# Slot bias carried by the logits weights, and the weights prepared inside the attention stage

## The chip, the cores and the metric

The kernel runs on one core of one Trainium2 chip. The time is the device time of one execution in microseconds. Before the change three executions took 1048.29, 1049.57 and 1051.22 us, median 1049.57. The engines are named as in the profile: PE (TensorE), DVE (VectorE), ACT (ScalarE), POOL (GpSimd) and SP (SyncE, which here only issues transfers). A name such as SPq is an engine's queue of issues.

## The reference

Images are cut into 36 patches of 768 numbers and embedded into 256 features, 77 text tokens are put behind them, and then come an attention layer and a soft mixture of experts, each with a layernorm and a residual:

```python
h = patches @ W.T + b                       # 32 x 36 x 256
h = concatenate([h, txt], axis=1)           # 32 x 113 x 256
h = h + attention(layernorm(h))             # 16 heads of 16, rotary embedding
x = layernorm(h)
logits = x @ phi_w.T + phi_b                # 3616 tokens x 64 experts x 32 slots
D = softmax(logits over the 32 slots)
C = softmax(logits over the 64 experts)
X = D^T x, clipped, normalised, tanh        # 2048 slots x 256
Y = X @ expert_w + expert_b                 # per expert
out = h + C Y
```

`phi_w` is 2048 x 256 and `phi_b` has 2048 entries (one bias for each slot of each expert).

## The kernel before, in words

The program has three stages, each a block of its own with a barrier behind it: no engine begins a stage before all engines and all awaited transfers of the last are done.

`embed` multiplies the patches, nine tiles of 128 rows. While it runs, ACT issues the loads of the weights of the later stages: the query-key, value and output projections and `phi`, which arrives as 128 partitions of 2 x 2048 numbers (KC = 2 halves of 128 features). Each of these is split into two parts, a high part rounded to fp32r by ACT (`hi`, L126) and the rest (`lo`): POOL computes it at L133, and for the second half of `phi` DVE does at L170. DVE also prepares the slot bias here: L161, L164 and L165 put its high part in row 0 and its low part in row 32 of `bias_rows`, whose other rows are zero. Behind each embedded tile DVE adds the token bias (L157) and SP stores the tile (L113). The block ends when the stores have landed and the split weights are there.

`attend` handles one batch element of 113 tokens per step, in a software pipeline: in step b element b+3 is normalised, b+2 is projected to queries and keys, b+1 is turned (transposed for the scores), b is scored, b-1 is finished and b-2 gets its residual. The first steps, b = -3 to 2, are written out, and then comes a loop. Within a step every engine follows its own fixed order. POOL's is: variance plus epsilon (L383), inverse root (L385), then the sums of the rotary embedding into `attend_stack` (L395). DVE's normalisation (L339) waits for L385, and it stands ahead of the rotary products (L347, L350) in DVE's order. PE transposes the normalised rows (L551) behind it. SP loads the input rows of an element, 36 from the embedding and 77 from the text, two steps ahead, each load waiting for L339 to be done with the buffer it refills.

`slots` handles 29 tiles (the first of 32 tokens, the others of 128). For a tile PE computes the logits in four banks of 512 columns: per bank one product of `bias_ones` with `bias_rows` (L1115) and six products of the two halves of the high and low parts (L1118). For the first five tiles (`early`) all four banks stand ahead of the group products (L1092) in PE's order; after that they are woven between the transposes of the weights (L1083). DVE takes the maxima (L811), subtracts them (L816), sums (L800, L845) and collects the products (L792, L794); POOL subtracts and scales whole tiles (L929, L933, L937); ACT copies and exponentiates. Behind the tiles come the experts and the combination of the outputs.

Of the kernel before, what the change touches and what calls it, by code (L numbers as in the profile page):

```python
# [29 lines left out]
KC = C // 128  # L30
# [46 lines left out]
def embed(nc, patches, wt, bias_row, emb, loads, identity, ident, slot_bias_row, bias_rows, bias_ones):  # L77
# [4 lines left out]
    with ExitStack() as ctx:  # L82
# [7 lines left out]
        slot_raw, slot_hi = sb("slot_raw", [64, E]), sb("slot_hi", [64, E], F32R)  # L90
# [3 lines left out]
        ident_in, slot_in = sem("ident_in"), sem("slot_in")  # L94
        slot_zero_ok, slot_hi_ok, slot_ok = sem("slot_zero_ok"), sem("slot_hi_ok"), sem("slot_ok")
        raw_in = [sem(f"raw_in{n}") for n in range(len(loads))]
        hi_done, lo_done, half_done = sem("hi_done"), sem("lo_done"), sem("half_done")
# [19 lines left out]
        @block.scalar  # L117
        def _(act):
            act.wait_ge(px_in[tiles - 2], 16)
            act.dma_start(slot_raw[:], slot_bias_row.broadcast_to([64, E])).then_inc(slot_in, 16)  # L120
            act.dma_start(ident[:], identity).then_inc(ident_in, 16)
            for n, (src, _, _) in enumerate(loads):
                act.dma_start(raw[n][:], src).then_inc(raw_in[n], 16)
            for n, (_, hi, _) in enumerate(loads):
                act.wait_ge(raw_in[n], 16)
                nc.scalar.activation(hi[:], raw[n][:], ACT.Copy).then_inc(hi_done, 1)  # L126

        @block.gpsimd
        def _(pool):
            for n, (_, hi, lo) in enumerate(loads):  # L130
                pool.wait_ge(hi_done, n + 1)
                part = slice(0, KC // 2) if n == len(loads) - 1 else slice(0, KC)
                nc.gpsimd.tensor_tensor(lo[:, part], raw[n][:, part], hi[:, part].bitcast(F32),  # L133
                                        ALU.subtract).then_inc(lo_done, 1)
            pool.wait_ge(lo_done, len(loads))
# [38 lines left out]

def attend(nc, emb, txt, rope_cos, rope_sin, ident, wqk, wv, wo, h2):
# [8 lines left out]
    with ExitStack() as ctx:  # L184
# [28 lines left out]

        p_score = pb("p_score", [T, GH, 512])
# [11 lines left out]
        tables_in = sem("tables_in")  # L226
        h_ld = [sem("h_ld0"), sem("h_ld1")]
# [37 lines left out]
        def _(sp):  # L265
# [7 lines left out]
            sp.dma_start(sin[:], rope_sin).then_inc(tables_in, 16)  # L273

# [95 lines left out]
        def _(pool):  # L370
# [8 lines left out]
            def step(b, half, par, flags):  # L379
# [18 lines left out]
            steps(pool, step)  # L398
            pool.wait_ge(stack_ok, 2 * BATCH)

        @block.scalar
        def _(act):
# [9 lines left out]
            def step(b, half, par, flags):  # L412
# [152 lines left out]
def slots(nc, h2, phi, slot_bias, ident, xacc, eb, y_parts, ct_dram, ebias, wexp, w_slots, out):  # L565
# [6 lines left out]
    bias_rows, bias_ones = slot_bias  # L572
    with ExitStack() as ctx:
# [15 lines left out]
        xn = [sb(f"xn{i}", [128, C]) for i in range(2)]  # L589
# [22 lines left out]
        xst = [t[:].rearrange("p (k c) -> p k c", k=KC) for t in xn]  # L612
# [155 lines left out]
        def _(dve):  # L768
            nc.vector.memset(eps[:], EPS)
            nc.vector.memset(e_power[:], -0.5)  # L770
            nc.vector.memset(power[:], -0.5).then_inc(consts, 1)
# [8 lines left out]
            def norm_end(n, par, rows):  # L780
# [3 lines left out]
                nc.vector.tensor_scalar(xn[par][0:rows], h_t[par][0:rows], mv[0:rows, 0:1], rstd[0:rows],  # L784
# [186 lines left out]
        def _(act):  # L971
# [9 lines left out]
            def step(t, half, c):  # L981
# [9 lines left out]
                if live:  # L991
# [3 lines left out]
                    nc.scalar.activation(x[c % RING][0:rows], xn[c % 2][0:rows], ACT.Copy).then_inc(kept_ok, 1)  # L995
# [66 lines left out]
        def _(pe):  # L1062
            def turn_x(t, c, nrows):
# [3 lines left out]
                for k in range(KC):  # L1067
                    last = nc.tensor.transpose(p_turn[0][:, k, 0:nrows], xn[(c + 1) % 2][0:nrows, 128 * k:128 * k + 128],
# [38 lines left out]
            def multiply_logits(t, nrows, banks):  # L1107

                pe.wait_ge(xt_lo_ok, val(t + 2))
                for b in banks:  # L1110
# [97 lines left out]
def program(nc, patches, txt, wt, tok_b, wqk, wv, wo, phi, phi_b, wexp, ebias, rope_cos, rope_sin, identity, out):  # L1208
# [7 lines left out]
    with (nc.sbuf_tensor("ident", [128, 128], F32) as ident, ExitStack() as whole):  # L1216
# [7 lines left out]
        bias_rows = whole.enter_context(nc.sbuf_tensor("bias_rows", [128, E], F32R))  # L1224
        bias_ones = whole.enter_context(nc.sbuf_tensor("bias_ones", [128, 128], F32R))
        with ExitStack() as projections:
# [3 lines left out]
            embed(nc, patches, wt, tok_b, emb, [(wqk, *wqk_parts), (wv, *wv_parts), (wo, *wo_parts),  # L1230
                                                (phi, *phi_parts)], identity, ident, phi_b, bias_rows, bias_ones)
            attend(nc, emb, txt, rope_cos, rope_sin, ident, wqk_parts, wv_parts, wo_parts, h2)
        slots(nc, h2, phi_parts, (bias_rows, bias_ones), ident, xacc, eb, y_parts, ct, ebias, wexp, w_slots, out)
# [41 lines left out]
```

## Time and profile before

| what | value |
| --- | --- |
| median of 3 runs | 1049.57 us |
| the profiled execution, its own time | 1050.74 us |
| its span, first to last instruction | 1049.0 us |
| busy: PE, DVE, ACT, POOL | 953.9, 752.7, 483.3, 459.6 us |
| mean granted TensorE clock, 1.00 being 2.4 GHz | 0.958 |
| moved by transfers | 110.42 MB |

The durations below come from that one profiled execution, whose own time is 1.74 us more than its span and 1.17 us more than the median. Busy shares are means over stages with different limits, so each stage has to be read by itself: `embed` ends near 42 us, `attend` near 340, the tiles of `slots` near 814. Matmuls are pipelined, so that PE reads as busy also where each product merely overlaps the next.

### The profile page before, as it was taken

How to read it: one execution, taken by the hardware profiler on the slowest of the kernel's cores; microseconds unless marked ns; L12 is line 12 of the kernel's file. 1: busy time of each engine (PE TensorE's matmuls, PEld its weight loads, DVE VectorE, ACT ScalarE, POOL GpSimd, SP SyncE). 2: the span in 40 equal slices, each digit the busy share in tenths (PEclk: the TensorE clock that was granted, in tenths of full speed). 3: DMA queues.
4: the chain of work that ended last, by engine and by line, in shares of the span. 5: the costliest groups of instructions: out<-in, count | busy, mean ns of one | idle time of the engine just before them, and what ended most of it. 6: DMA issues, size and time to landing. Idle time of an engine off the chain costs nothing.

```text
span 1049.0 us, 22748 instructions
## 1 busy us (share of the span) xinstructions
PE 953.9 (91%) x8338; PEld 809.2 (77%) x8338; DVE 752.7 (72%) x1095; ACT 483.3 (46%) x768; POOL 459.6 (44%) x375
## 2 busy tenths in 40 slices
PE   7389999999997558799999999999998997999997
PEld 6278888887885346688887888888887756999997
DVE  1746767667663398899998999999998553544442
ACT  1145555555553144565565565566556233333331
POOL 0422222222220077687786787777777341010100
PEclk9689999999998788999999999999999998999999
DMA  9201111111110402223323223323325894776660
GB/s 303 73 21 36 42 42 42 40 41 40 41 33 29 103 10 56 58 79 92 80 61 88 68 67 90 82 60 86 91 62 180 318 410 145 236 224 240 220 201 23
DMA packets 97688, 110.42 MB, mean 105 GB/s; under 512 B 12148, under 2 KB 88980, under 8 KB 91684
## 3 DMA queue, kind: packets, MB, share of 16 engines
q1 hardware_dynamic: 95460, 102.31, 31.7%
q10 hardware_dynamic: 800, 3.74, 1.0%
q0 software_dynamic: 1376, 3.70, 0.9%
q8 instruction: 29, 0.48, 0.2%
q14 instruction: 23, 0.19, 0.1%
HBM read 71.51 MB, written 38.21 MB: 105 GB/s over the span
## 4 chain that ended last, share of the span: by engine, by line
DVE 26%; PE 24%; issue 11%; POOL 3%; ACT 2%; DVEq 0%; DMA 0%; POOLq 0%; ACTq 0%
PE slots_p_turn L1200 15%; DVE slots_dmax L811 6%; DVE slots_csum L800 6%; DVE slots_dsum L845 5%; PE slots_p_sum L1092 3%; DVE slots_disp L816 3%; PE slots_logits L1118 3%; DVE xacc L794 3%; ACT slots_comb L1004 1%; PE slots_logits L1167 1%; POOL slots_comb L929 1%; POOL slots_disp L933 1%; DVE slots_xn L784 1%; DVE slots_xt_lo L828 1%; DVE slots_cmax L839 1%
## 5 line engine op out<-in xcount | busy, mean ns | idle before, releaser
L1092 PE MATMUL slots_p_sum<-slots_x,slots_disp 128*128 128x256 f32 (+1 forms) x928 | 208.1, 382 | 6.1 <-POOL slots_disp L933 6.1
L1092 PEld LDWEIGHTS slots_p_sum<-slots_x,slots_disp 128*128 128x128 f32 (+1 forms) x928 | 174.6, 191 | 31.3 <-POOL slots_disp L933 4.7
L937 POOL TENSOR_TENSOR slots_comb<-slots_comb,slots_csum 128x2048 f32<-128x2048 f32 (+1 forms) x29 | 105.0, 3619 | 66.0 <-DVE slots_csum L802 66.0
L929 POOL TENSOR_TENSOR slots_comb<-slots_comb,slots_cmax 128x1024 f32<-128x1024 f32 (+1 forms) x58 | 112.0, 1949 | 44.1 <-DVE slots_cmax L839 44.1
L933 POOL TENSOR_TENSOR slots_disp<-slots_disp,slots_dsum 128x2048 f32<-128x2048 f32 (+1 forms) x29 | 105.8, 3647 | 0.0
L1004 ACT ACTIVATE slots_comb<-slots_logits 128x512 f32<-128x512 f32 (+1 forms) x116 | 66.1, 598 | 85.3 <-DVE slots_disp L816 85.3
L816 DVE TENSOR_TENSOR slots_disp<-slots_logits,slots_dmax 128x512 f32<-128x512 f32 (+1 forms) x116 | 80.2, 691 | 5.9 <-issue 1.9
L964 POOL DMA_DIRECT2D out<-slots_o x29 | 15.9, 548 | 156.3 <-DVE slots_o L899 156.3
L395 POOL TENSOR_TENSOR attend_stack<-attend_rope_a,attend_rope_b 113x256 f32<-113x256 f32 x64 | 45.3, 729 | 88.9 <-DVE attend_rope_b L350 88.9
L978 ACT ACTIVATE slots_ct<-slots_p_turn 128x512 f32<-128x512 f32 (+1 forms) x116 | 64.1, 580 | 38.7 <-PE slots_p_turn L1083 38.6
L811 DVE TENSOR_REDUCE slots_dmax<-slots_logits 128x16 f32<-128x512 f32 (+1 forms) x116 | 78.8, 679 | 3.3 <-PE slots_logits L1118 1.8
L989 ACT ACTIVATE slots_comb<-slots_comb 128x1024 f32<-128x1024 f32 (+1 forms) x58 | 61.5, 1060 | 33.4 <-POOL slots_comb L929 33.3
L1118 PE MATMUL slots_logits<-phi_hi,slots_xt_hi 128*128 128x512 f32 (+1 forms) x232 | 75.6, 408 | 0.0
L1118 PE MATMUL slots_logits<-phi_hi,slots_xt_lo 128*128 128x512 f32 (+1 forms) x232 | 75.3, 407 | 0.0
L1118 PE MATMUL slots_logits<-phi_lo,slots_xt_hi 128*128 128x512 f32 (+1 forms) x232 | 74.9, 405 | 0.0
L311 DVE TENSOR_REDUCE attend_stack<-attend_p_score 113x16 f32<-113x1808 f32 x32 | 65.4, 2043 | 13.2 <-PE attend_p_score L459 13.2
L1115 PE MATMUL slots_logits<-bias_rows,bias_ones 128*128 128x512 f32 (+1 forms) x116 | 54.4, 469 | 19.3 <-DVE slots_xt_lo L828 18.2
L409 ACT ACTIVATE attend_prob_t<-attend_p_score 113x904 f32<-113x904 f32 x64 | 55.7, 923 | 28.7 <-PE attend_p_score L468 28.7
L800 DVE TENSOR_REDUCE slots_csum<-slots_comb 128x32 f32<-128x2048 f32 (+1 forms) x29 | 66.0, 2277 | 3.3 <-ACT slots_comb L989 3.3
L839 DVE TENSOR_REDUCE slots_cmax<-slots_comb 128x32 f32<-128x2048 f32 (+1 forms) x29 | 66.3, 2286 | 2.8 <-ACT slots_comb L1004 1.3
L1083 PE MATMUL slots_p_turn<-ident,slots_comb 128*128 128x128 f32 (+1 forms) x464 | 63.7, 272 | 2.6 <-POOL slots_comb L937 1.5
L845 DVE TENSOR_REDUCE slots_dsum<-slots_disp 128x64 f32<-128x2048 f32 (+1 forms) x29 | 66.1, 2279 | 0.0
(132 smaller groups left out, 1973.6 us busy)
## 6 DMA issues: line engine op xcount, KB each, us to landing
combine_t<-slots_ct SPq DMA_DIRECT2D x224, 128.0 KB, 2.4
slots_comb<-combine_t SPq DMA_DIRECT2D x14, 1024.0 KB, 5.6
slots_ct<-combine_t SPq DMA_DIRECT2D x14, 1024.0 KB, 5.8
expert_w<-wexp SPq DMA_DIRECT2D x8, 1024.0 KB, 9.1
slots_disp<-wexp SPq DMA_DIRECT2D x8, 1024.0 KB, 13.4
h<-attend_h_out SPq DMA_DIRECT2D x32, 113.0 KB
slots_h_t<-h SPq DMA_DIRECT2D x28, 128.0 KB, 2.2
slots_x<-h SPq DMA_DIRECT2D x28, 128.0 KB, 2.0
```

The lines of the kernel that those rows point to most:

```text
L800: nc.vector.reduce_sum(csum[0:rows, 0], comb[par % 2][0:rows], AX_X).then_inc(csum_ok, 1)
L811: nc.vector.reduce_max(dmax[0:rows, bank(b)], logits[0:rows, bank(b), :], AX_X).then_inc(dmax_ok, 1)
L816: nc.vector.tensor_tensor(disp[c % RING][0:rows, bank(b), :], logits[0:rows, bank(b), :], dmax[0:rows, bank(b)].unsqueeze(2).broadcast_to( ...
L839: nc.vector.reduce_max(cmax[0:rows], comb[c % 2][0:rows], AX_X).then_inc(cmax_ok, 1)
L845: nc.vector.reduce_sum(dsum[0:rows, 0], disp[c % RING][0:rows], AX_X).then_inc(dsum_ok, 1)
L929: nc.gpsimd.tensor_tensor(m, m, cmax[0:rows, shalf(i)].unsqueeze(2).broadcast_to([rows, SLOTS // 2, EXPERTS]), ALU.subtract).then_inc(csub ...
L933: nc.gpsimd.tensor_tensor(d, d, dsum[0:rows, 1].unsqueeze(2).broadcast_to([rows, EXPERTS, SLOTS]), ALU.mult).then_inc(disp_ok, 1)
L937: nc.gpsimd.tensor_tensor(m, m, csum[0:rows, 1].unsqueeze(2).broadcast_to([rows, SLOTS, EXPERTS]), ALU.mult).then_inc(comb_ok, 1)
L1004: nc.scalar.activation(comb[c % 2][0:rows, :, bank(b)], logits[0:rows, bank(b), :].rearrange("p n s -> p s n"), ACT.Copy).then_inc(copied_ ...
L1092: last = nc.tensor.matmul(p_sum[u % 2][:, i, :], disp[d][0:rows].rearrange("p n s -> p (n s)")[:, 128 * e:128 * e + 128], x[d][0:rows], st ...
L1118: last = nc.tensor.matmul(out_b, a[:, k, 0:nrows], wt[:, k, cols], start=False, stop=i == 2 and k == KC - 1)
L1200: last = nc.tensor.matmul(p_o[c % 2][0:rows], a[c % 2][:, e, 0:rows], part[:, e, :], start=k == 0, stop=k == 3 * EB - 1)
```

## The change

The normalised token row has mean zero over its 256 features, so the first feature is minus the sum of the others. Subtracting the weights of the first feature from all the others therefore lets the first feature be left out of the product. The 255 remaining features and a column of ones make 256 rows again, and the weight row that meets the ones is the slot bias. `xn` in `slots` gets a 257th column of ones, the transposes read columns 1 to 256, and the product of the bias is gone, with `bias_rows`, `bias_ones` and all that filled them.

The weights `phi` are no longer loaded and split in `embed`. In `attend` SP loads them, shifted by one feature: 127 partitions of 16 KB, two single rows (feature 128 and the bias) into partition 127, and the row of the first feature broadcast over 128 partitions. In steps -2 to 1 POOL subtracts the first row from a quarter of the weights, at the end of a step ACT rounds the high part of a quarter (steps -1 to 2), and POOL subtracts for the low part (steps -1 to 2). POOL's first subtraction waits for all four transfers.

```diff
@@ embed
-            act.dma_start(slot_raw[:], slot_bias_row.broadcast_to([64, E])).then_inc(slot_in, 16)
             act.dma_start(ident[:], identity).then_inc(ident_in, 16)
...
-                part = slice(0, KC // 2) if n == len(loads) - 1 else slice(0, KC)
-                nc.gpsimd.tensor_tensor(lo[:, part], raw[n][:, part], hi[:, part].bitcast(F32),
-                                        ALU.subtract).then_inc(lo_done, 1)
+                nc.gpsimd.tensor_tensor(lo[:], raw[n][:], hi[:].bitcast(F32), ALU.subtract).then_inc(lo_done, 1)
...
-            nc.vector.memset(bias_rows[:].bitcast(F32), 0.0)
-            nc.vector.memset(bias_ones[:].bitcast(F32), 1.0).then_inc(slot_zero_ok, 1)
...
-                if t == tiles - 3:
-
-                    dve.wait_ge(slot_in, 16)
-                    nc.vector.tensor_copy(slot_hi[:], slot_raw[:]).then_inc(slot_hi_ok, 1)
-                    dve.wait_ge(slot_hi_ok, 1)
-                    dve.wait_ge(slot_zero_ok, 1)
-                    nc.vector.tensor_copy(bias_rows[0:1], slot_raw[0:1]).then_inc(slot_ok, 1)
-                    nc.vector.tensor_tensor(bias_rows[32:33], slot_raw[32:33], slot_hi[32:33].bitcast(F32),
-                                            ALU.subtract).then_inc(slot_ok, 1)
-            dve.wait_ge(slot_ok, 2)
-            dve.wait_ge(hi_done, len(loads))
-            _, hi, lo = loads[-1]
-            nc.vector.tensor_tensor(lo[:, KC // 2:KC], raw[-1][:, KC // 2:KC], hi[:, KC // 2:KC].bitcast(F32),
-                                    ALU.subtract).then_inc(half_done, 1)
-            dve.wait_ge(half_done, 1)
@@ attend
+        PIECES = 4
+        piece = lambda t, i: t[:].rearrange("p k e -> p (k e)")[:, i * KC * E // PIECES:(i + 1) * KC * E // PIECES]
...
             sp.dma_start(sin[:], rope_sin).then_inc(tables_in, 16)
+            sp.dma_start(phi_raw[0:127], phi[1:128]).then_inc(phi_in, 16)
+            sp.dma_start(phi_raw[127:128, 0], phi[0:1, 1]).then_inc(phi_in, 16)
+            sp.dma_start(phi_raw[127:128, 1], slot_bias).then_inc(phi_in, 16)
+            sp.dma_start(phi_first[:], phi[0:1, 0].broadcast_to([128, E])).then_inc(phi_in, 16)
...
+                if isinstance(b, int) and -2 <= b < PIECES - 2:
+
+
+                    pool.wait_ge(phi_in, 64)
+                    i = b + 2
+                    rows = slice(0, 128 if i < PIECES // KC else 127)
+                    part = slice(i * KC * E // PIECES % E, i * KC * E // PIECES % E + KC * E // PIECES)
+                    nc.gpsimd.tensor_tensor(piece(phi_raw, i)[rows], piece(phi_raw, i)[rows], phi_first[rows, part],
+                                            ALU.subtract).then_inc(phi_sub_ok, 1)
+                if isinstance(b, int) and -1 <= b < PIECES - 1:
+
+                    pool.wait_ge(phi_hi_ok, b + 2)
+                    nc.gpsimd.tensor_tensor(piece(phi_lo, b + 1), piece(phi_raw, b + 1), piece(phi_hi, b + 1).bitcast(F32),
+                                            ALU.subtract).then_inc(phi_lo_ok, 1)
...
+                if isinstance(b, int) and -1 <= b < PIECES - 1:
+
+                    act.wait_ge(phi_sub_ok, b + 2)
+                    nc.scalar.activation(piece(phi_hi, b + 1), piece(phi_raw, b + 1), ACT.Copy).then_inc(phi_hi_ok, 1)
@@ slots
-        xn = [sb(f"xn{i}", [128, C]) for i in range(2)]
+        xn = [sb(f"xn{i}", [128, C + 1]) for i in range(2)]
...
+            for i in range(2):
+                nc.vector.memset(xn[i][:, C:C + 1], 1.0)
...
-                    last = nc.tensor.transpose(p_turn[0][:, k, 0:nrows], xn[(c + 1) % 2][0:nrows, 128 * k:128 * k + 128],
+                    last = nc.tensor.transpose(p_turn[0][:, k, 0:nrows], xn[(c + 1) % 2][0:nrows, 128 * k + 1:128 * k + 129],
                                                ident[0:nrows, 0:nrows])
...
-                    nc.tensor.matmul(out_b, bias_ones[:, 0:nrows], bias_rows[:, cols], start=True, stop=False)
                     for i, (a, wt) in enumerate(((xt_hi, phi_hi), (xt_hi, phi_lo), (xt_lo, phi_hi))):
                         for k in range(KC):
-                            last = nc.tensor.matmul(out_b, a[:, k, 0:nrows], wt[:, k, cols], start=False,
+                            last = nc.tensor.matmul(out_b, a[:, k, 0:nrows], wt[:, k, cols], start=i == 0 and k == 0,
                                                     stop=i == 2 and k == KC - 1)
```

What SP issues at the start of `attend` in the changed kernel, in its order (`attend_h_in` are the input rows, a bracket names the semaphore that an issue waits for):

```order
L256 DMA attend_cos<-rope_cos 113x16
L257 DMA attend_sin<-rope_sin 113x16
L258 DMA attend_phi_raw<-phi 127x4096
L259 DMA attend_phi_raw<-phi 1x2048
L260 DMA attend_phi_raw<-phi_b 1x2048
L261 DMA attend_phi_first<-phi 128x2048
L251 DMA attend_h_in<-emb 36x256 [waits attend_xn_ok]
L252 DMA attend_h_in<-txt 77x256
```

The four issues with `phi` are new and stand ahead of the loads of elements 2 and 3. Before the change the loads stood directly behind the two tables.

What POOL has in steps -2 and -1 in the kernel before (`attend_mv` and `attend_rstd` are the variance and inverse root of the element to be normalised):

```order
L383 TENSOR_TENSOR attend_mv<-attend_mv,attend_eps 113x1 [waits attend_mv_ok]
L385 TENSOR_TENSOR attend_rstd<-attend_mv,attend_power 113x1 [waits attend_var_ok]
L395 TENSOR_TENSOR attend_stack<-attend_rope_a,attend_rope_b 113x4x4x16 [waits attend_rope_ok]
L395 TENSOR_TENSOR attend_stack<-attend_rope_a,attend_rope_b 113x4x4x16
L383 TENSOR_TENSOR attend_mv<-attend_mv,attend_eps 113x1 [waits attend_mv_ok]
L385 TENSOR_TENSOR attend_rstd<-attend_mv,attend_power 113x1 [waits attend_var_ok]
L395 TENSOR_TENSOR attend_stack<-attend_rope_a,attend_rope_b 113x4x4x16 [waits attend_rope_ok]
```

And in the changed kernel, in the same steps and the start of step 0:

```order
L371 TENSOR_TENSOR attend_mv<-attend_mv,attend_eps 113x1 [waits attend_mv_ok]
L373 TENSOR_TENSOR attend_rstd<-attend_mv,attend_power 113x1 [waits attend_var_ok]
L383 TENSOR_TENSOR attend_stack<-attend_rope_a,attend_rope_b 113x4x4x16 [waits attend_rope_ok]
L383 TENSOR_TENSOR attend_stack<-attend_rope_a,attend_rope_b 113x4x4x16
L392 TENSOR_TENSOR attend_phi_raw<-attend_phi_raw,attend_phi_first 128x1024 [waits attend_phi_in]
L371 TENSOR_TENSOR attend_mv<-attend_mv,attend_eps 113x1 [waits attend_mv_ok]
L373 TENSOR_TENSOR attend_rstd<-attend_mv,attend_power 113x1 [waits attend_var_ok]
L383 TENSOR_TENSOR attend_stack<-attend_rope_a,attend_rope_b 113x4x4x16 [waits attend_rope_ok]
L383 TENSOR_TENSOR attend_stack<-attend_rope_a,attend_rope_b 113x4x4x16
L392 TENSOR_TENSOR attend_phi_raw<-attend_phi_raw,attend_phi_first 128x1024 [waits attend_phi_in]
L397 TENSOR_TENSOR phi_lo<-attend_phi_raw,phi_hi 128x1024 [waits attend_phi_hi_ok]
L371 TENSOR_TENSOR attend_mv<-attend_mv,attend_eps 113x1 [waits attend_mv_ok]
```

Between the rotary sums of element 0 and the inverse root of element 2 there is now the subtraction that waits for the transfers; from step -1 on two operations over 1024 columns stand there.

## Rows read from the trace of the kernel before

**Rows 1.** Busy time by stage: stretch, length, each engine (instructions), clock, transfer share, GB/s.
```profile
0.00:42.00 42.00, 25.39 (x108) 21.45 (x108) 19.21 (x15) 7.00 (x5) 11.45 (x8) 0.92 0.65 224
42.00:340.00 298.00, 276.88 (x4288) 226.76 (x4288) 191.75 (x390) 150.16 (x288) 70.93 (x132) 0.95 0.12 37
...
348.00:458.00 110.00, 82.74 (x358) 61.53 (x359) 92.41 (x125) 49.32 (x83) 67.83 (x39) 0.87 0.25 60
458.00:798.00 340.00, 336.77 (x1703) 286.10 (x1702) 328.36 (x415) 196.18 (x308) 257.82 (x131) 1.00 0.29 76
```

**Rows 2.** End of `embed` and start of `attend`, in order of time: start, length, engine, line.
```profile
24.74 6.21 PE L146 MATMUL embed_acc<-embed_wt_sb,embed_px 128*128 128x256 f32 x28
...
30.02 3.24 DVE L165 TENSOR_TENSOR bias_rows<-embed_slot_raw,embed_slot_hi 1x2048 fp32r<-1x2048 f32 x1
...
34.96 6.62 DVE L170 TENSOR_TENSOR phi_lo<-embed_raw,phi_hi 128x2048 fp32r<-128x2048 f32 x1 [0.91 <-ACT phi_hi L126]
42.07 0.95 POOL L372 MEMSET attend_stack<- 113x1024 f32 x1 [2.65 <-POOLq L82]
```

**Rows 3.** Stores of the embedded tiles in 28 to 36 us, KB each, us to landing.
```profile
emb<-embed_emb_sb SPq DMA_DIRECT2D x2, 128.0 KB, 1.8
```

**Rows 4.** SP, POOL, DVE and PE in the first steps of `attend`, in order of time.
```profile
43.97 0.62 SPq L273 DMA_DIRECT2D attend_sin<-rope_sin  x1
...
52.78 1.41 POOL L395 TENSOR_TENSOR attend_stack<-attend_rope_a,attend_rope_b 113x256 f32<-113x256 f32 x2 [2.98 <-DVE attend_rope_b L350]
...
54.42 0.55 POOL L385 TENSOR_TENSOR attend_rstd<-attend_mv,attend_power 113x1 f32<-113x1 f32 x1
...
55.01 0.41 DVE L339 TENSOR_SCALAR attend_xn<-attend_h_in,attend_mv,attend_rstd 113x256 f32<-113x256 f32 x1 [1.40 <-POOL attend_rstd L385]
...
59.57 0.36 PE L551 MATMUL attend_p_row<-ident,attend_xn 113*128 113x113 f32 x2
```

**Rows 5.** Transfers in 44.9 to 47 us, of which 226 packets are the two 113-row tables.
```profile
DMA packets 235, 0.02 MB, mean 8 GB/s; under 512 B 232, under 2 KB 235, under 8 KB 235
```

**Rows 6.** Transfers in 339 to 348 us: the last 113-row stores.
```profile
DMA packets 198, 0.21 MB, mean 23 GB/s; under 512 B 2, under 2 KB 197, under 8 KB 197
...
q1 hardware_dynamic: 197, 0.20, 6.2%
...
h<-attend_h_out SPq DMA_DIRECT2D x1, 113.0 KB
```

**Rows 7.** Transfers in 24 to 31.5 us; q10 is ACT's queue, then loading `phi`.
```profile
q10 hardware_dynamic: 125, 1.72, 54.3%
```

**Rows 8.** ACT and PE in step 0 of `attend`, in order of time.
```profile
69.57 0.37 ACT L447 ACTIVATE attend_xt_hi<-attend_p_row 128x226 fp32r<-128x226 f32 x1
70.40 0.55 ACT L417 ACTIVATE attend_ot_sb<-attend_p_k 128x452 f32<-128x452 f32 x1 [0.46 <-PE attend_p_k L479]
```

**Rows 9.** Costliest groups: line, operation, count, busy, mean ns, idle before.
```profile
L929 POOL TENSOR_TENSOR slots_comb<-slots_comb,slots_cmax 128x1024 f32<-128x1024 f32 (+1 forms) x58 | 112.0, 1949 | 44.1 <-DVE slots_cmax L839 44.1
...
L1115 PE MATMUL slots_logits<-bias_rows,bias_ones 128*128 128x512 f32 (+1 forms) x116 | 54.4, 469 | 19.3 <-DVE slots_xt_lo L828 18.2
```

**Rows 10.** The chain of waits in 350 to 470 us: start, us, what; one early tile.
```profile
393.11 0.79 PE slots_logits L1115
393.90 2.56 PE slots_logits L1118 x6
396.46 0.43 PE slots_logits L1115
...
398.56 0.23 PE slots_logits L1115
398.80 1.39 PE slots_logits L1118 x6
```

**Rows 11.** Waits of DVE in 350 to 458 us: us in total, times, longest.
```profile
DVE xacc L792 <- PE slots_p_sum L1092: 4.4, 8, 1.2
...
DVE slots_csum L800 <- ACT slots_comb L989: 2.2, 3, 0.7
```

More of the change, by code:

```diff
@@ L74, in head_of, with embed @@
     return 8 * (g // 2) + 2 * j + g % 2
-def embed(nc, patches, wt, bias_row, emb, loads, identity, ident, slot_bias_row, bias_rows, bias_ones):
+def embed(nc, patches, wt, bias_row, emb, loads, identity, ident):
     tiles = BATCH * PATCHES // 128
@@ L89, in embed @@
         raw = [sb(f"raw{n}", list(hi.shape)) for n, (_, hi, _) in enumerate(loads)]
-        slot_raw, slot_hi = sb("slot_raw", [64, E]), sb("slot_hi", [64, E], F32R)
         acc = [ctx.enter_context(nc.psum_tensor(f"embed_acc{i}", [128, C], F32)) for i in range(BANKS)]
@@ L93, in embed @@
         w_in, b_in = [sem("tok_w_in0"), sem("tok_w_in1")], sem("tok_b_in")
-        ident_in, slot_in = sem("ident_in"), sem("slot_in")
-        slot_zero_ok, slot_hi_ok, slot_ok = sem("slot_zero_ok"), sem("slot_hi_ok"), sem("slot_ok")
+        ident_in = sem("ident_in")
         raw_in = [sem(f"raw_in{n}") for n in range(len(loads))]
-        hi_done, lo_done, half_done = sem("hi_done"), sem("lo_done"), sem("half_done")
+        hi_done, lo_done = sem("hi_done"), sem("lo_done")
         mm_done, emb_ready, emb_out = sem("emb_mm"), sem("emb_ready"), sem("emb_out")
@@ L157, in _, with attend @@
                 nc.vector.tensor_tensor(emb_sb[:, t], acc[t % BANKS][:], bias[:], ALU.add).then_inc(emb_ready, 1)
-                if t == tiles - 3:
-                    dve.wait_ge(slot_in, 16)
-                    nc.vector.tensor_copy(slot_hi[:], slot_raw[:]).then_inc(slot_hi_ok, 1)
-                    dve.wait_ge(slot_hi_ok, 1)
-                    dve.wait_ge(slot_zero_ok, 1)
-                    nc.vector.tensor_copy(bias_rows[0:1], slot_raw[0:1]).then_inc(slot_ok, 1)
-                    nc.vector.tensor_tensor(bias_rows[32:33], slot_raw[32:33], slot_hi[32:33].bitcast(F32),
-                                            ALU.subtract).then_inc(slot_ok, 1)
-            dve.wait_ge(slot_ok, 2)
-            dve.wait_ge(hi_done, len(loads))
-            _, hi, lo = loads[-1]
-            nc.vector.tensor_tensor(lo[:, KC // 2:KC], raw[-1][:, KC // 2:KC], hi[:, KC // 2:KC].bitcast(F32),
-                                    ALU.subtract).then_inc(half_done, 1)
-            dve.wait_ge(half_done, 1)
-def attend(nc, emb, txt, rope_cos, rope_sin, ident, wqk, wv, wo, h2):
+def attend(nc, emb, txt, rope_cos, rope_sin, ident, wqk, wv, wo, phi, slot_bias, phi_parts, h2):
     (wqk_hi, wqk_lo), (wv_hi, wv_lo), (wo_hi, wo_lo) = wqk, wv, wo
@@ L212, in attend @@
         ont_lo = sb("ont_lo", [128, KC, T], F32R)
+        phi_hi, phi_lo = phi_parts
+        phi_raw, phi_first = sb("phi_raw", [128, KC, E]), sb("phi_first", [128, E])
+        PIECES = 4
+        piece = lambda t, i: t[:].rearrange("p k e -> p (k e)")[:, i * KC * E // PIECES:(i + 1) * KC * E // PIECES]
         p_score = pb("p_score", [T, GH, 512])
@@ L226, in attend @@
         tables_in = sem("tables_in")
+        phi_in, phi_sub_ok, phi_hi_ok, phi_lo_ok = sem("phi_in"), sem("phi_sub_ok"), sem("phi_hi_ok"), sem("phi_lo_ok")
         h_ld = [sem("h_ld0"), sem("h_ld1")]
@@ L396, in step @@
                                                 ALU.add).then_inc(stack_ok, 1)
+                if isinstance(b, int) and -2 <= b < PIECES - 2:
[9 more added lines that the diff above has]
+                                            ALU.subtract).then_inc(phi_lo_ok, 1)
             steps(pool, step)
             pool.wait_ge(stack_ok, 2 * BATCH)
+            pool.wait_ge(phi_lo_ok, PIECES)
         @block.scalar
@@ L562, in _, with slots @@
             steps(pe, step)
-def slots(nc, h2, phi, slot_bias, ident, xacc, eb, y_parts, ct_dram, ebias, wexp, w_slots, out):
+def slots(nc, h2, phi, ident, xacc, eb, y_parts, ct_dram, ebias, wexp, w_slots, out):
     phi_hi, phi_lo = phi
-    bias_rows, bias_ones = slot_bias
     with ExitStack() as ctx:
@@ L611, in slots @@
         WRING = len(w)
-        xst = [t[:].rearrange("p (k c) -> p k c", k=KC) for t in xn]
+        xst = [t[:, 0:C].rearrange("p (k c) -> p k c", k=KC) for t in xn]
         y = [t[:] for t in h_t]
@@ L783, in norm_end @@
                 wait_for(dve, xt_ps_ok, n - 1)
-                nc.vector.tensor_scalar(xn[par][0:rows], h_t[par][0:rows], mv[0:rows, 0:1], rstd[0:rows],
+                nc.vector.tensor_scalar(xn[par][0:rows, 0:C], h_t[par][0:rows], mv[0:rows, 0:1], rstd[0:rows],
                                         ALU.subtract, ALU.mult).then_inc(x_ok, 1)
@@ L994, in step @@
                         act.wait_ge(sum_ok, val(summed_before(t, c)))
-                    nc.scalar.activation(x[c % RING][0:rows], xn[c % 2][0:rows], ACT.Copy).then_inc(kept_ok, 1)
+                    nc.scalar.activation(x[c % RING][0:rows], xn[c % 2][0:rows, 0:C], ACT.Copy).then_inc(kept_ok, 1)
                 if nxt:
@@ L1223, in program @@
         w_slots = [whole.enter_context(nc.sbuf_tensor(f"expert_w{i}", [128, EPB, KC, C], F32))[:] for i in range(2 * KC)]
-        bias_rows = whole.enter_context(nc.sbuf_tensor("bias_rows", [128, E], F32R))
-        bias_ones = whole.enter_context(nc.sbuf_tensor("bias_ones", [128, 128], F32R))
         with ExitStack() as projections:
@@ L1229, in program @@
             wo_parts = parts(projections, "wo", [128, KC, C])
[L1230 to L1233, printed above, removed]
+            embed(nc, patches, wt, tok_b, emb, [(wqk, *wqk_parts), (wv, *wv_parts), (wo, *wo_parts)],
+                      identity, ident)
+            attend(nc, emb, txt, rope_cos, rope_sin, ident, wqk_parts, wv_parts, wo_parts, phi, phi_b, phi_parts, h2)
+        slots(nc, h2, phi_parts, ident, xacc, eb, y_parts, ct, ebias, wexp, w_slots, out)
 def kernel(x, txt, L0_tok_W, L0_tok_b, L0_attn_Wq, L0_attn_Wk, L0_attn_Wv, L0_attn_Wo, L0_ffn_phi_w, L0_ffn_phi_b,
```

## The prediction

> **What bounds the kernel now.** I read the busy times by stage first, then each stage by itself. The tiles of `slots` are the largest stage: in 340 us of it DVE is busy 328.36 and PE 336.77 [rows 1]. Both look full, but the two figures don't mean the same. PE's busy time counts overlapping products; DVE's operations stand end to end, so that stage can shrink by at most 340 − 328.36 = 11.6 us, however much PE is relieved. In the 110 us ahead of it (first tiles) DVE is busy only 92.41 and PE runs at a mean clock of 0.87 [rows 1]; there the chain of waits goes through the logits products [rows 10], and DVE waits for PE [rows 11]. In `embed` the end is not set by PE, whose last product ends at 24.74 + 6.21 = 30.95, but by the preparation of slot bias and `phi`: DVE works at L165 until 33.3 and at L170 from 34.96 to 41.58, and the next block begins at 42.07 [rows 2]. In `attend` PE is busy 276.88 of 298 us [rows 1] and the engines wait for each other in a short cycle, so a wait that stops POOL stops all.
>
> **The end of `embed`: earlier.** DVE's bias work and both halves of the split of `phi` go. The last embedded tile is added 0.45 us behind PE's last product, at 31.4. Its store lands 1.8 us behind its issue where little else moves [rows 3], so at 33.3. The barrier took 42.07 − 41.58 = 0.5 us [rows 2]. `attend` begins at 33.8 instead of 42.07, 8.3 us earlier. This gain isn't simply kept, as the next step shows.
>
> **The four new transfers.** SP issues them behind the tables, whose last issue ended at 43.97 + 0.62 = 44.6, 2.5 us into the block [rows 4]. The big one has 127 rows of 16,384 bytes, 2.08 MB. How many of the 16 transfer engines share it decides everything. In the 9 us at the end of `attend` only stores of 113 rows move: 197 packets use 6.2% of 16 engines, which is one engine of 16 (6.25%), at 23 GB/s [rows 6]. In the same way the two tables, loads of 113 rows, take from about 44.9 to 46.6 us for 226 packets of 64 bytes at 9 GB/s, one behind the other [rows 5]; spread over 16 engines they would be gone in a tenth of that. 113 is a prime number, and so is 127; 128 rows, as `phi` had them, kept 54.3% of all engines busy for 7.5 us [rows 7]. So I take the 127-row load to run on a single engine.
>
> The Trainium skill, on the page "DMA: Bandwidth & Descriptors" (section "Why a DMA increments its semaphore by 16 and not by 1"), says that the number of engines is the largest up to 16 that divides the slowest dimension of both sides, and names 127 partitions as a case with one engine. No row here shows a transfer of 127 rows; the rows of 113 agree with the rule.
>
> Its duration: ACT's queue moved 1.72 MB of `phi` and its neighbours with 0.543 × 16 × 7.5 = 65.2 us of engine time, 26.4 GB/s for one engine [rows 7]. That gives 2.08 MB / 26.4 = 78.8 us. The other end is the measured single engine with 1 KB rows, 23 GB/s [rows 6]: 90 us. The load's rows are long and come from the same array as those of rows 7, so I take 78.8. The tables are served before it: they ended near 46.6, 4.5 us into the block, so it runs from 33.8 + 4.5 = 38.3 to 117.1. Behind it on the same engine lie that engine's eight rows of the broadcast first row (8 × 8 KB, 2.5 us) and the two single rows (0.6 us): 120.2, and with the release some 120.5.
>
> **Who waits.** POOL's first subtraction stands behind the rotary sums of step -2, which ended at 52.78 + 1.41 = 54.2, or 12.1 us into the block [rows 4]. In the changed kernel POOL is there at 45.9 and waits about 74.6 us. Queued behind it on POOL is the inverse root of element 2 (L385); for that waits DVE's normalisation (L339), behind which the rotary products of element 1 stand, and PE's transposes. Also the input rows of elements 2 and 3 are issued behind the big load and have to share that one engine. Nothing but the rest of PE's step -1 runs meanwhile.
> After the release: the subtraction over 1024 columns, between 1949 ns (a like POOL operation, [rows 9]) and 2.35 us, say 2.2; variance and root 0.8; the normalisation 0.41 [rows 4]: PE's transposes L551 start at 123.9. Before they started at 59.57 [rows 4], held by PE's own work, which is done by then. The shift is **+64.3 us**, the 8.3 us of `embed` already inside.
>
> **The rest of the preparation.** In steps -1 to 2 POOL gets up to two operations of 2.0 to 2.2 us more per step of about 9 us. POOL is busy 70.93 of 298 us in `attend` [rows 1], so I cost them at nothing; the cover is POOL's wait for the rotary products, and without it each step would be 2 us late. ACT gets four roundings of about 1.06 us (the first in the shadow of the stall). In step 0 it has 70.40 − (69.57 + 0.37) = 0.46 us free before the copy that PE waits for next [rows 8], so three steps are up to 0.6 us late: +1.5 us (0 to 3).
>
> **The bias products.** They have 54.4 us of busy time in 116 products [rows 9]. In the bulk of the tiles this frees PE, not DVE: I take 0 there, at best the 11.6 us above. In the first tiles they are on the chain. A tile shows 0.79, 0.43, 0.23 and 0.23 us for them, 1.68 together [rows 10] (the second 0.23 is that of the fourth bank). But the first bank takes 2.56 us against 1.39 in the last, that is, the first bank runs at the lower of the clock's two levels (1.2 GHz) and the last at 2.4, and the rise comes while the products run; taking products out puts others into the slow stretch, so that only 4 × 0.23 = 0.92 us is sure. Five tiles have their logits on the chain (the first and those of steps 1 to 4): between 4.6 and 8.4 us. DVE waited 4.4 + 2.2 us there for the group products and the exponentials that follow [rows 11]. I take −5.5.
>
> **Other edits.** The 257th column, the two tiny fills, the shifted transposes and the removed semaphores cost nothing that the rows could show.
>
> **The sum.** 64.3 + 1.5 − 5.5 = +60.3 on the span of 1049.0 gives 1109.3. The execution's own time lies 1.74 above its span, 1111.0; the median of the runs lies 1.17 below that execution, so **1110 us**.
>
> **The rivals.**
> - *The load is spread over the engines* (the shape is cut in another way than the 113-row transfers, which nothing in the rows suggests). `embed` moved 224 GB/s at a share of 0.65 [rows 1], 345 GB/s at full use; 3.1 MB take 9 us. Issued at 36.3, all lands near 47.5, POOL waits 1.6 us and its subtraction delays the root by 3.8 us, most of it under PE's 4.4 us of work. Then −8.3 + 1 + 1.5 − 5.5 = −11.3: 1038 us, faster. The load decides the sign once it lands more than about 12 us later than that. Chance 0.09.
> - *The tiles gain too*: PE's busy 99% is the true bound there. Against it: DVE is busy 328.36 of the 340 us. At most −11.6 on the forecast: 1098 to 1103 us. Chance 0.04.
> - *The clock falls in the tiles*, since PE, idle 3.2 us in 340 now [rows 1], gets a pause of some 0.9 us more in each. If PE fell to 1.2 GHz in each of 22 tiles for as long as in the tile of [rows 10] (393.1 to some 396.6), it would lose 1.75 us and have 0.92 spare: 22 × 0.8 = +18, 1128 us. Against it: the pauses remain short beside those of the first tiles, where it does fall. Chance 0.03.
> - *The load is slower*, at 23 GB/s: +11, 1121 us. This is the upper part of my own case.
>
> **Numbers.** My case has 0.84, its own range is 1100 to 1122 (load 26.4 to 23 GB/s, ACT 0 to 3 us, first tiles −4.6 to −8.4). The range 1097 to 1123 takes in the second rival and leaves out the first and the third. Faster by over 0.3% (about what this kernel's runs can tell from none) 0.09, within 0.3% 0.01, slower 0.90.
>
> **What would show it.** In the profile after: `attend` begins near 34; a DMA row at one engine's share, about 0.06, from 38 to 120 us, at some 26 GB/s; POOL's longest wait, some 75 us, ahead of the first subtraction; PE, DVE and ACT nearly empty there; the tile period of the bulk unchanged at DVE's pace; first tiles about 1.1 us shorter. The prediction is wrong if the transfer share in that stretch is far above one engine's, or if the root of element 2 does not stand behind the wait.

## The result and the profile after

The changed kernel takes 1116.21 us (median of four runs, 1116.07 to 1118.22) against 1049.03 for the kernel before: 1.064 times as long, 95% interval 1.062 to 1.066. The forecast was 1110, range 1097 to 1123. The profiled execution took 1116.07 us with a span of 1114.4.

The busy times by stage, with the columns of [rows 1]. `attend` now begins at 33.8 and its stall fills the second row; the third is the rest of `attend`, the fourth the first tiles, the fifth the bulk.

```profile
0.00:34.00 34.00, 25.71 (x108) 21.71 (x108) 3.92 (x11) 3.38 (x4) 5.22 (x8) 1.00 0.59 199
34.00:121.00 87.00, 8.52 (x30) 6.19 (x30) 5.06 (x15) 2.20 (x5) 4.70 (x10) 0.55 0.11 41
121.00:407.00 286.00, 271.36 (x4252) 222.96 (x4252) 185.77 (x371) 151.13 (x286) 84.56 (x130) 0.95 0.13 37
415.00:521.00 106.00, 75.26 (x311) 54.88 (x312) 87.69 (x119) 45.79 (x78) 63.16 (x38) 0.79 0.27 63
521.00:862.00 341.00, 324.81 (x1628) 272.98 (x1627) 330.07 (x418) 195.81 (x309) 259.51 (x131) 0.99 0.29 76
```

From 34 to 121 us PE is busy for 8.5 us of 87, the clock is at its lower level most of the time, and the transfer share is 0.11. The loss arises there. Of that stretch, the 28 us from 47 to 75, in which nothing but the big load moves, in the view of transfers, which answers to [rows 6]:

```profile
DMA packets 46, 0.75 MB, mean 27 GB/s; under 512 B 0, under 2 KB 0, under 8 KB 0
...
q1 hardware_dynamic: 46, 0.75, 6.3%
```

46 packets of 16 KB in 28 us are 6.3% of 16 engines, 27 GB/s: one engine, as 113 rows had been. POOL's longest waits between 30 and 140 us (line, for whom, us in total, times, longest):

```profile
POOL attend_phi_raw L392 <- DMA attend_phi_first<-phi: 75.9, 1, 75.9
```

And in order of time, start and length first, what stands around that wait; these answer to [rows 2, 4]:

```profile
33.77 1.84 POOL L360 MEMSET attend_stack<- 113x1024 f32 x2 [7.05 <-POOLq L82]
...
37.50 36.95 SPq L259 DMA_DIRECT2D attend_phi_raw<-phi  x1
...
44.51 1.41 POOL L383 TENSOR_TENSOR attend_stack<-attend_rope_a,attend_rope_b 113x256 f32<-113x256 f32 x2 [2.98 <-DVE attend_rope_b L338]
```

```profile
121.85 2.34 POOL L392 TENSOR_TENSOR attend_phi_raw<-attend_phi_raw,attend_phi_first 128x1024 f32<-128x1024 f32 x1 [75.92 <-DMA attend_phi_first<-phi]
122.23 0.43 DVE L322 BATCH_NORM_STATS2 attend_stats<-attend_h_in 113x6 f32<-113x256 f32 x1 [77.50 <-DMA attend_h_in<-txt]
...
124.42 0.55 POOL L373 TENSOR_TENSOR attend_rstd<-attend_mv,attend_power 113x1 f32<-113x1 f32 x1
125.00 0.41 DVE L327 TENSOR_SCALAR attend_xn<-attend_h_in,attend_mv,attend_rstd 113x256 f32<-113x256 f32 x1 [2.07 <-POOL attend_rstd L373]
...
125.47 0.64 PE L558 MATMUL attend_p_row<-ident,attend_xn 113*128 113x113 f32 x2 [74.83 <-DVE attend_xn L327]
...
130.46 2.36 POOL L397 TENSOR_TENSOR phi_lo<-attend_phi_raw,phi_hi 128x1024 fp32r<-128x1024 f32 x1
```

POOL ends its rotary sums at 45.9 and subtracts at 121.85. DVE's statistics of element 2 waited just as long, 77.5 us, for their own row loads. SP's second new issue took 36.95 us: SP stood still until about half the big load had gone. The inverse root comes behind the subtraction, then DVE, then PE's transposes at 125.47, where they were at 59.57 before [rows 4]: +65.9.

In the first tiles the chain of waits (start, us, what) has one entry per tile where [rows 10] had eight. The first tile and the one that answers to the tile of [rows 10]:

```profile
422.80 8.46 PE slots_logits L1125 x24
...
461.83 7.93 PE slots_logits L1125 x24
469.77 1.92 PE slots_p_sum L1100 x8
```

DVE's waits there answer to [rows 11]: for the group products they fell from 4.4 to 1.7 us, for the exponentials they rose from 2.2 to 2.6.

```profile
DVE slots_csum L808 <- ACT slots_comb L997: 2.6, 3, 1.1
...
DVE xacc L800 <- PE slots_p_sum L1100: 1.7, 6, 0.4
```

### The profile page after: what moved, and what is told of

Its sections match the earlier page's. It is cut to its first block, busy times and chain, and to the rows that moved or that the text cites. A ratio compares the mean times of both kernels' runs of the same rounds, so it can differ in the third digit from the quotient of the medians.

```text
span 1114.4 us, 22522 instructions
## 1 busy us (share of the span) xinstructions
PE 940.6 (84%) x8222; PEld 793.1 (71%) x8222; DVE 737.0 (66%) x1091; ACT 481.3 (43%) x771; POOL 471.6 (42%) x382
## 3 DMA queue, kind: packets, MB, share of 16 engines
q1 hardware_dynamic: 95736, 105.46, 30.7%
## 4 chain that ended last, share of the span: by engine, by line
PE 26%; DVE 20%; issue 7%; POOL 7%; ACT 2%; DMA 0%; DVEq 0%; POOLq 0%; ACTq 0%
PE slots_p_turn L1207 14%; PE slots_logits L1125 5%; DVE slots_csum L808 5%; DVE slots_dmax L819 4%; PE slots_p_sum L1100 4%; DVE slots_disp L824 3%; DVE slots_dsum L853 3%; POOL slots_comb L937 2%; POOL slots_disp L941 2%; POOL slots_comb L945 2%; DVE slots_cmax L847 2%; PE slots_logits L1174 1%; PE slots_p_turn L1091 1%; DVE xacc L802 1%; ACT slots_comb L1012 1%
## 5 line engine op out<-in xcount | busy, mean ns | idle before, releaser
L1100 PE MATMUL slots_p_sum<-slots_x,slots_disp 128*128 128x256 f32 (+1 forms) x928 | 212.8, 388 | 15.7 <-POOL slots_disp L941 15.7
L1100 PEld LDWEIGHTS slots_p_sum<-slots_x,slots_disp 128*128 128x128 f32 (+1 forms) x928 | 177.7, 194 | 42.8 <-POOL slots_disp L941 10.4
L1125 PE MATMUL slots_logits<-phi_hi,slots_xt_hi 128*128 128x512 f32 (+1 forms) x232 | 83.5, 442 | 19.8 <-DVE slots_xt_lo L836 18.8
L558 PE MATMUL attend_p_row<-ident,attend_xn 113*128 113x113 f32 x64 | 12.2, 274 | 82.9 <-DVE attend_xn L327 82.8
L299 DVE TENSOR_REDUCE attend_stack<-attend_p_score 113x16 f32<-113x1808 f32 x32 | 65.4, 2043 | 15.6 <-PE attend_p_score L466 15.4
L1091 PEld LDWEIGHTS slots_p_turn<-ident,slots_comb 128*128 128x128 f32 (+1 forms) x464 | 53.3, 142 | 23.8 <-POOL slots_comb L945 11.8
```

Of the source, the lines that this page charges most:

```text
L1091: last = nc.tensor.transpose(p_turn[q % 2][:, i, 0:rows], weights[:, 128 * e:128 * e + 128], ident[0:rows, 0:rows])
L1100: last = nc.tensor.matmul(p_sum[u % 2][:, i, :], disp[d][0:rows].rearrange("p n s -> p (n s)")[:, 128 * e:128 * e + 128], x[d][0:rows], st ...
```

## The experiments

All are compared with the kernel before, run on the same chip in the same job.

**Cut the load into 112 and 15 rows.**

```diff
-            sp.dma_start(phi_raw[0:127], phi[1:128]).then_inc(phi_in, 16)
+            sp.dma_start(phi_raw[0:112], phi[1:113]).then_inc(phi_in, 16)
+            sp.dma_start(phi_raw[112:127], phi[113:128]).then_inc(phi_in, 16)
...
-                    pool.wait_ge(phi_in, 64)
+                    pool.wait_ge(phi_in, 80)
```

> The changed kernel, with the load of 127 rows cut into one of 112 rows (16 times 7) and one of 15. If the stall is the one engine that carried 127 rows, 3 MB now move at some 300 to 400 GB/s, land 9 us behind their issue at 36.5, and POOL waits under 3 us instead of 75.9: 1041 us (1036 to 1046), faster than the kernel before. If the stall comes from the work itself (POOL's and ACT's preparation, or the volume of 3 MB), the time stays above 1100.

Measured: 1047.3 us, ratio 0.998 (0.996 to 1.000). One more transfer and one other constant give back 69 us, so the stall is the way in which 127 rows are carried and nothing in POOL's or ACT's work. But the time lies above the expected range (1036 to 1046): POOL still waits 7.5 us, and a packet of 16 KB takes 1031 ns in the median, where it took 612 in the changed kernel. Busy times of the stretch in which the load runs:

```profile
38.00:46.00 8.00, 3.90 (x10) 2.42 (x10) 3.39 (x9) 0.72 (x2) 2.16 (x5) 0.50 1.04 253
```

All 16 transfer engines are busy (the share of 1.04 is a rough figure, since it cannot exceed 1), yet they move 253 GB/s.

**Cut it into 124 and 3 rows**: `phi_raw[0:124]` and `phi_raw[124:127]`, otherwise the same edit.

> The changed kernel with the load cut into 124 rows (4 times 31) and 3 rows. If the number of engines is the largest one that divides the rows, 124 rows run on 4 engines, 31 rows of 16 KB each: at 26 to 28 GB/s per engine 18 to 19 us instead of 75. POOL is released near 60 and waits some 15 us: 1055 us (1050 to 1060). If only the prime number 127 is a special case and 124 rows go over all engines, it comes out like the cut into 112 and 15, near 1041.

Measured: 1070.8 us (1063.1 to 1071.4), ratio 1.016 (1.011 to 1.022), between the two others and above the expected range. From 54 to 68 us the share stays at about a quarter, which is four engines of 16, as expected for 124 rows; but POOL waited 28.6 us, not 15, since four engines together moved 71 GB/s (47 to 68 us), 18 each, against 27 for the single one:

```profile
DMA packets 121, 1.50 MB, mean 71 GB/s; under 512 B 8, under 2 KB 31, under 8 KB 31
...
q1 hardware_dynamic: 121, 1.50, 25.7%
```

**The preparation late, the load as it is.** All POOL and ACT operations of the preparation in steps 29 to 33:

```diff
+        LATE = BATCH - 1
...
-                if isinstance(b, int) and -2 <= b < PIECES - 2:
+                if isinstance(b, int) and LATE - 2 <= b < LATE + PIECES - 2:
...
-                if isinstance(b, int) and -1 <= b < PIECES - 1:
+                if isinstance(b, int) and LATE - 1 <= b < LATE + PIECES - 1:
```

> The changed kernel with the same load of 127 rows, but with all eight POOL and four ACT operations of the preparation moved from steps -2 to 2 to steps 29 to 33 of the attention, so that POOL meets no wait for the load in the first steps. Theory 1, POOL's wait is what stalls the stage: the load lands under the running steps, 1041 us (1036 to 1048). Theory 2, the row loads of elements 2 and 3 behind the big load (issued by SP only at 76 to 91 us and sharing its one engine) stall the stage as well: DVE's statistics of element 2 still begin near 122, and it stays at 1110 to 1116 us.

Measured: 1112.1 us, ratio 1.058 (1.054 to 1.061). This is theory 2. POOL's wait, which I had named as the place of the stall, is one of two that ended within half a microsecond of each other. Without it DVE waits as long for the rows of element 2:

```profile
DVE attend_stats L323 <- DMA attend_h_in<-txt: 77.8, 2, 76.9
```

**The same, with the 127 rows issued by ACT** ahead of its first wait in `attend`:

> The kernel with the preparation moved to steps 29 to 33 (1112 us), with the load of 127 rows issued by ACT, on its own queue, instead of SP; the three small ones stay with SP. Theory 1, with the preparation late the stall came from SP's queue: SP was held for 36 us at the next issue, and the row loads stood in the same ring behind the 127 rows. Then the stall goes though the big load still takes 78 us on one engine: 1041 us (1037 to 1046). Theory 2, whatever shares that transfer engine is stalled, on which queue it may be: the row loads again arrive near 120 us, 1105 to 1115.

Measured: 1111.8 us, ratio 1.059 (1.057 to 1.061). This is theory 2 in its time, but other transfers were held up than it named. On ACT's queue the load starts before the tables of 113 rows, which use the same one engine. SP stood for 41 us at its issue of the second table, and DVE waited for that:

```profile
DVE attend_rope_a L335 <- DMA attend_sin<-rope_sin: 60.2, 1, 60.2
```

```profile
35.38 41.09 SPq L258 DMA_DIRECT2D attend_sin<-rope_sin  x1
```

So neither a later use nor another queue frees the small transfers that need the same engine. A 127-row load issued later, behind the row loads of elements 2 and 3, was not run.

**Cut it into 120 and 7 rows**, since a cut into blocks of 8 rows might restore the rate:

> The changed kernel with the load cut into 120 rows (15 times 8) and 7 rows. With 112 and 15 rows the packets of 16 KB took 1031 ns in the median, with 31 rows on each of 4 engines up to 1218 ns, against 611 ns where each of 16 engines had 8 rows of 128 (before) or one engine had all (the changed kernel). Theory 1, an engine has the full rate as long as it keeps to its own block of 8 partitions: 611 ns here, the 120 rows are in after 5 us, POOL waits 2 to 4 us instead of 7.5, and the time is 1043 us. Theory 2, the rows that several engines read at once compete anyway: packets stay near 1 us and the time at 1047.

Measured: 1047.2 us, ratio 0.999 (0.997 to 1.000), POOL waits 8.2 us. Theory 1 fell: packets of 16 KB took 1265 ns in the median, so 15 engines with 8 rows each are no faster than 16 with 7.

**One load of 128 rows.** The input is laid out with features 1 to 255 and the bias as its last row, and the first feature's row takes the place of the bias input:

```diff
-            sp.dma_start(phi_raw[0:127], phi[1:128]).then_inc(phi_in, 16)
-            sp.dma_start(phi_raw[127:128, 0], phi[0:1, 1]).then_inc(phi_in, 16)
-            sp.dma_start(phi_raw[127:128, 1], slot_bias).then_inc(phi_in, 16)
-            sp.dma_start(phi_first[:], phi[0:1, 0].broadcast_to([128, E])).then_inc(phi_in, 16)
+            sp.dma_start(phi_raw[:], phi).then_inc(phi_in, 16)
+            sp.dma_start(phi_first[:], slot_bias.broadcast_to([128, E])).then_inc(phi_in, 16)
```

> The changed kernel with the shift by one feature and the bias row already in the layout of the input, so that one load of 128 rows and the broadcast of the first feature's row replace the four transfers. Theory 1 (own block of 8 partitions): packets of 611 ns, some 5 us for the load and 5 to 6 us for the broadcast, POOL waits 2 to 4 us; 1042 us (1038 to 1045). Theory 2 (reads compete anyway): like the cut into 112 and 15, 1047.

Measured: 1042.7 us, ratio 0.994 (0.992 to 0.995), POOL waits 1.5 us. The packets of 16 KB took 611 ns in the median. Time and packets are as expected, though the reason given, blocks of 8, had fallen at the same moment.

**What costs the rate.** The two loads differ in the shift of the source by one row and in the rows per engine. Two kernels take these apart: the cut into 112 and 15 without the shift (it reads the wrong features), and 128 rows with one:

```diff
-            sp.dma_start(phi_raw[0:112], phi[1:113]).then_inc(phi_in, 16)
+            sp.dma_start(phi_raw[0:112], phi[0:112]).then_inc(phi_in, 16)
```

> The kernel with the load cut into 112 and 15 rows, but reading rows 0 to 111 and 112 to 126 of the source instead of rows 1 to 127; its weights are therefore those of the wrong features. Its packets of 16 KB took 1031 ns in the median, those of the 128-row load 611. Theory 1, the shift of the source by one row costs the rate: 611 ns here, POOL waits 2 to 4 us, 1043 us. Theory 2, the number of rows per engine (7, or 8 on 15 engines, instead of 8 on 16) costs it: packets stay near 1 us, 1047 us.

> The kernel with one load of 128 rows (1042.7 us, packets of 611 ns), but with one row of zeros put ahead in the input, so that the load reads rows 1 to 128 of 129: the same shift of the source by 16 KB as in the changed kernel, with 8 rows on each of 16 engines. Theory 1 (the shift of the source): packets near 1 us, POOL waits 7 us, 1047 us. Theory 2 (the rows per engine): 611 ns, 1042.7 us.

Measured: 1045.9 us with 112 rows (ratio 0.997, 0.996 to 0.999, POOL waits 6.1 us) and 1042.2 with 128 shifted rows (0.994, 0.993 to 0.996, 1.8 us). The same stretch in both, share and GB/s in the last two columns:

```profile
38.00:46.00 8.00, 3.90 (x10) 2.42 (x10) 3.39 (x9) 0.72 (x2) 2.15 (x5) 0.50 1.03 258
```

```profile
38.00:46.00 8.00, 3.90 (x10) 2.42 (x10) 3.39 (x9) 0.72 (x2) 2.17 (x4) 0.63 0.97 372
```

At full share one moves 258 GB/s and the other 372 (in its last 2 us or so packets of 8 KB of the broadcast run too). The packets of 16 KB alone took 987 and 611 ns in the median. The shift by one row doesn't matter: 128 rows run at 611 ns with it and without. What does matter is the cut: only one load of 128 rows, 8 on each of 16 engines, ran at the full rate. The cut loads have fewer rows on an engine and also a second load behind them; these two were not separated, and why the other cuts run slower stays open.

**The bias product alone**, removed from the kernel before (L1115 gone, the first product of L1118 starts the sum; the slot bias is left out):

> The kernel before without the product of the bias in the logits; the slot bias is left out of the computation, its preparation stays. This is the part of the gain in the tiles by itself. My sum had -5.5 us (-4.6 to -8.4): 1043.5. The profile of the changed kernel shows some -2.4 in the first tiles and -0.8 at a turn of the loop, since TensorE's clock is low for longer there: 1046. If PE bounded the bulk of the tiles, it would be up to 20 us: 1029.

Measured: 1046.9 us, ratio 0.997 (0.996 to 0.999), −2.8 us. That is far from the 20 us of the bulk bounded by PE, so PE did not bound it.

**The version that the runs point to**: 128 rows and the broadcast, issued by SP behind its step 2, and the preparation late.

```diff
+        LATE = BATCH - 1
...
             for b in range(-3, 3):
                 step(b, None, b % 2, [0 <= b + n < BATCH for n in (3, 2, 1, 0, -1, -2)])
+            sp.dma_start(phi_raw[:], phi).then_inc(phi_in, 16)
+            sp.dma_start(phi_first[:], slot_bias.broadcast_to([128, E])).then_inc(phi_in, 16)
```

> All of it: the input laid out shifted (one load of 128 rows and a broadcast), issued by SP behind its step 2, and the preparation in steps 29 to 33. Nothing waits for the weights in the first steps. Attention begins 8 us earlier and the tiles are 2.5 to 4 us shorter, with at most 1 us lost in the last steps: 1039 us (1035 to 1043), faster than the kernel before. If the transfers of 3 MB delay the row loads of steps 4 to 6, up to 5 us come back.

Measured: 1040.3 us (1037.1 to 1041.2), ratio 0.991 (0.989 to 0.993). It beats both kernels. Its four runs lie below the four of the 128-row load with the early preparation (1042.2 to 1043.1); but the 128 shifted rows, the same work in another job, ran from 1040.3 to 1047.3, so the 2.3 us between the two medians, and with it the worth of the late preparation, is not certain.

## Why the prediction was right, step by step

The mechanism and the sign were right. The sum was 5.1 us short on the span, and 6.2 on the medians: I had taken off 1.17 us for the distance of the profiled execution from the median, and after the change that distance was nothing (1116.07 against 1116.21). The terms on the span, from the same operations in the profiles before and after:

| step | forecast | measured |
| --- | --- | --- |
| `attend` begins | 33.8 | 33.77 |
| POOL released | 120.5 | 121.85 |
| PE's transposes of element 2 | +64.3 | +65.9 |
| rest of the preparation | +1.5 | +1.3 |
| last steps of `attend` | 0 | +2.8 |
| first tiles | −5.5 | −2.3 |
| bulk of the tiles | 0 | −0.8 |
| behind the tiles | 0 | −1.5 |
| sum | +60.3 | +65.4 |

The last steps of `attend` and the first tiles make the largest part of the miss. The small terms are uncertain, since each is the difference of two single executions: the kernel without the bias product has the `attend` of the kernel before, unchanged, and finished it 1.7 us sooner. No run explains the −1.5 behind the tiles. My own range was also added up wrongly: the bounds that I name give 1106 to 1124, not 1100 to 1122; the measured time lies in both.

*The engine count.* From 113 rows I read that a prime number of rows runs on one engine, and the load did. The Trainium skill's page "DMA: Bandwidth & Descriptors" (section "Why a DMA increments its semaphore by 16 and not by 1") gives the number of engines as the largest up to 16 that divides the slowest dimension of both sides. The traces agree: shares of 6.3% with 127 rows and about a quarter with 124. The duration by [rows 7] was right too, 27 GB/s for 26.4. The release came 1.35 us later; SP's stall of 36.95 us at its next issue, which I did not foresee, kept the broadcast back until 76 us. It then went through the other engines quickly:

```profile
76.00:80.00 4.00, 0.00 (x0) 0.00 (x0) 0.00 (x0) 0.00 (x0) 0.00 (x0) 0.50 0.69 264
84.00:112.00 28.00, 0.00 (x0) 0.00 (x0) 0.00 (x0) 0.00 (x0) 0.00 (x0) 0.50 0.08 33
```

From 84 us on the share is near that of one engine again, at the big load, with packets of the row loads beside it.

*Who waits.* I put the stall on POOL's wait and only mentioned the row loads. The late preparation shows that the row loads alone are enough for the stall; whether POOL's wait alone would be was not run. After the release the normalisation came 2.07 us behind DVE's statistics, because the subtraction (2.34 us, where I took 2.2) stood between them; in the late version the transposes start 1.5 us earlier, at 124.00.

*The rest of the preparation.* The +1.3 us arise in steps -1 to 2 and are near the forecast, but partly by luck: I had put them on ACT and nothing on POOL. They come probably less from ACT than from POOL, whose operations took 2.34 to 2.39 us, at my upper bound of 2.35 where I had taken 2.0 to 2.2, so that the pair stands between the inverse roots. In the late version, without these operations, the same steps gain 1.7 us more; no run takes POOL's share and ACT's apart. DVE waited 3.00 us for the root ahead of the next normalisation:

```profile
133.04 0.55 POOL L373 TENSOR_TENSOR attend_rstd<-attend_mv,attend_power 113x1 f32<-113x1 f32 x1
...
133.63 0.41 DVE L327 TENSOR_SCALAR attend_xn<-attend_h_in,attend_mv,attend_rstd 113x256 f32<-113x256 f32 x1 [3.00 <-POOL attend_rstd L373]
```

*Last steps of `attend`.* They are unchanged code and took 2.8 us more, because PE's clock fell earlier: in the 6 us that begin with the rows below (390 to 396 us, before 323 to 329) the granted clock was 0.61 against 1.00, in the next 6 us 0.50 against 0.79. The products of probabilities and values took 1.71 us there, 1.32 before.

```profile
390.59 1.71 PE L486 MATMUL attend_p_k<-attend_prob_t,attend_vp 113*32 113x113 f32 x32 [0.79 <-ACT attend_prob_t L412]
```

```profile
323.44 1.32 PE L479 MATMUL attend_p_k<-attend_prob_t,attend_vp 113*32 113x113 f32 x32 [0.79 <-ACT attend_prob_t L409]
```

The version cut into 112 and 15 rows, with the same code there, lost only 0.4 us in these steps, and that with 120 and 7 lost 2.8. So the loss comes and goes between kernels with the same code there; what sets it is not shown.

*First tiles.* The term was mis-sized: −2.3 measured, less than my sure part of 4.6. I had counted 0.92 us for each of five tiles as the work taken out at full speed. Already the number was wrong: in the profile before, the logits of four tiles are on the chain (from 352.84, 376.34, 393.11 and 410.86), and in the profile after those of three (from 422.80, 461.83 and 478.81), with DVE's own operations in between. The 24 products of the tile at 461.83 take 7.93 us. Before, that tile's products began at 393.11 [rows 10] and ended with the last of these rows of its chain:

```profile
400.42 1.39 PE slots_logits L1118 x6
401.81 1.92 PE slots_p_sum L1092 x8
```

That is 8.70 us with the bias: 0.77 went, less than the 0.92, though products of 1.68 us were taken out. The first tile, 8.29 us before (352.84 to 361.13), now takes 8.46 and gained nothing; in the kernel without the bias product, where the same 24 products stand, it took 7.19. What differs is when the clock rises: in the changed kernel the first tile's products ran at the lower level for 6.0 us (422.80 to 428.77), in the kernel before for 3.4 (352.84 to 356.25). Over the stage PE is idle for 30.7 of 106 us, where it was for 27.3 of 110, and the mean clock fell from 0.87 [rows 1] to 0.79. The kernel without the bias product gives the same size for all tiles together, −2.8 us (−1.2 to −4.7 by the interval of its ratio).

*Bulk.* DVE's pace bounds it, as forecast: it is busy 330.07 of 341 us, PE 324.81, and without the bias product the time fell by 2.8 us in all. The −0.8 appears at one turn of the loop.

## What to carry to other kernels

Before a load is shifted by a row, look at the number of rows that is left: 127 put 2 MB on one of 16 transfer engines and cost 69 us against the cut into 112 and 15 and 74 against 128 rows, and the small transfers that needed that engine waited with it, on either queue. Lay the data out so that the load keeps 128 rows, and place its first use where it is long there. PE's busy share of 99% in the tiles said nothing of what its relief was worth; the engine to look at was the one whose operations stand end to end.

## What the hardware showed unexpectedly

- An issue can hold up the issuing engine: behind the 127-row load SP's next issue took 36.95 us, and one took 41.09 us when the load was on ACT's queue. What sets this time is not shown.
- The rate of one transfer engine depended on how the rows were divided. By the median time of a packet of 16 KB it was 27 GB/s alone (612 ns) and just as much on each of 16 with 8 rows (611 ns), but 17 on each of four with 31 rows (966 ns), 16 on each of 16 with 7 rows (1031 ns) and 13 on each of 15 with 8 rows (1265 ns).
- POOL's subtraction over 128 (or 127) x 1024 took 2.34 to 2.39 us in every instance of the changed kernel, and 1.95 for the operation with a broadcast operand in the tiles.
